# A last image gathered in four column parts, its row sums spread in float32r, and row sums transposed in bfloat16

## The reference

```
emb  = xn_flat @ dist_w.T                       # 1024 x 32
adj  = (24 nearest by distance) & (distance <= 10), or the diagonal
X    = xn_flat @ fc_w.T + fc_b
Dv   = row sums of adj;   De = column sums of adj
out  = (adj / De) @ adj.T / Dv @ X + xn_flat    # per image
o    = batch norm of out over all four images and all nodes, times gamma, plus beta
result = x + o * sigmoid(o)
```

## Time and profile before

| what | value |
|---|---|
| median of 3 runs | 173.52 us (173.44 to 174.02) |
| the profiled execution's own time | 173.63 us |
| its span (first to last instruction) | 171.8 us |
| busy: PE, DVE, ACT, POOL | 153.1, 143.6, 118.6, 105.7 us |
| mean granted TensorE clock | 0.974 of full speed |
| DMA | 17.72 MB, mean 103 GB/s |

### The profile page before, as it was taken

One profiled execution on the slowest core, in us unless ns is written; L12 is line 12 of the kernel. 1 busy time (PEld: TensorE's weight loads), 2 busy tenths in 40 slices (PEclk: granted clock), 3 DMA queues, 4 the chain that ended last, 5 costly groups with the idle time before them and its releaser, 6 DMA issues.

```text
span 171.8 us, 4074 instructions
## 1 busy us (share of the span) xinstructions
PE 153.1 (89%) x1235; PEld 98.9 (58%) x1237; DVE 143.6 (84%) x863; ACT 118.6 (69%) x199; POOL 105.7 (62%) x160
## 2 busy tenths in 40 slices
PE   6999999899989999899999989999999999999000
PEld 2334532444547665566666757667877778979000
DVE  0679999999996894999999999599769986588582
ACT  1257679998696996985578799649916574590590
POOL 1000556869975677399996479999619999380000
PEclk9999999999999999999999999999999999999955
DMA  5821000442937475309726070980641379994057
GB/s 191 264 111 2 2 4 0 63 74 52 121 68 126 51 77 109 78 12 200 113 52 122 4 123 4 214 154 6 122 92 37 62 184 95 148 338 163 0 208 280
DMA packets 42346, 17.72 MB, mean 103 GB/s; under 512 B 38832, under 2 KB 39496, under 8 KB 42320
## 3 DMA queue, kind: packets, MB, share of 16 engines
q1 hardware_dynamic: 41456, 17.03, 48.1%
q10 hardware_dynamic: 864, 0.40, 0.9%
HBM read 6.11 MB, written 2.13 MB: 48 GB/s over the span
## 4 chain that ended last, share of the span: by engine, by line
PE 72%; ACT 9%; DVE 6%; POOL 6%; issue 4%; ACTq 0%; DVEq 0%; POOLq 0%
PE pt L500 22%; PE pg L474 20%; PE po L533 10%; PE pt L562 5%; PE po L453 3%; ACT key L714 3%; PE po L431 3%; PE pt L533 2%; POOL x_wide L844 2%; DVE xn L1172 2%; PE po L440 2%; POOL tw L836 1%; ACT xn L800 1%; PE pg L555 1%; PE pg L453 1%
## 5 line engine op out<-in xcount | busy, mean ns | idle before, releaser
L982 DVE MAX8 cand<-key 128x8 f32<-128x64 f32 x512 | 78.1, 208 | 0.3
L500 PEld LDWEIGHTS pt<-xp,H 128*128 128x128 bf16 x768 | 44.4, 97 | 8.7 <-issue 7.6
L500 PE MATMUL pt<-xp,H 128*128 128x128 bf16 (+1 forms) x768 | 49.1, 220 | 0.1
L714 ACT ACTIVATE key<-pg 128x512 f32<-128x512 f32 x64 | 34.6, 594 | 19.1 <-PE pg L474 18.7
L474 PE MATMUL pg<-right,left 64*128 64x512 f32 x128 | 40.5, 641 | 3.1 <-ACT key L714 3.1
L881 POOL TENSOR_SCALAR H<-sign 128x1024 bf16<-128x1024 bf16 x32 | 33.4, 1043 | 13.1 <-ACT sign L722 13.1
L722 ACT ACTIVATE sign<-key,thr 128x1024 bf16<-128x1024 f32 x32 | 36.8, 1151 | 5.8 <-DVE thr L998 5.6
L474 PEld LDWEIGHTS pg<-right,left 64*128 64x128 f32 x128 | 12.5, 184 | 16.0 <-ACT key L714 8.0
L844 POOL CAST x_wide<-HT 128x1024 fp32r<-128x1024 bf16 x12 | 12.2, 1040 | 4.8 <-PE po L533 4.8
L562 PE MATMUL pt<-filler 128*128 128x512 bf16 x40 | 12.8, 450 | 1.4 <-POOL filler L805 1.3
L810 POOL TENSOR_SCALAR xn<-x_sb,gn_nm,gn_rs 128x1024 f32<-128x1024 f32 x3 | 3.6, 1194 | 16.4 <-DVE gn_rs L969 16.4
(11 more groups left out here) (96 smaller groups left out, 210.2 us busy)
## 6 DMA issues: line engine op xcount, KB each, us to landing
x_sb<-x SPq DMA_DIRECT2D x1, 2048.0 KB, 7.9
out<-xn SPq DMA_DIRECT2D x7, 256.0 KB, 2.1
dvb<-inv_rows SPq DMA_DIRECT2D x3, 512.0 KB, 4.5
x_sb<-x SPq DMA_DIRECT2D x1, 1024.0 KB, 6.4
left<-left SPq DMA_DIRECT2D x6, 128.0 KB, 2.3
x_sb<-x SPq DMA_DIRECT2D x1, 512.0 KB, 3.4
HT<-H SPq DMA_TRANSPOSE x32, 3.3
x_sb<-x ACTq DMA_DIRECT2D x1, 256.0 KB, 3.2
```

The source lines that it names most:

```text
L500: mm = pe.matmul(pt[:, j // T_BLOCKS, at:at + wide], lhs, x_cols(b, t, q, wide), start=(t == 0 and j % T_BLOCKS == 0 and q == 0), stop=(t ...
L714: act.activation(key[:, k % KEYS, cols], pg[:, h, :], ACT.Copy).then_inc(s["drained"], 1)
L982: ins = dve.max(cand[:, k % 2, c, :], key[:, k % KEYS, c * CHUNK:(c + 1) * CHUNK])
```

## The change

- The last image's gather has four parts of 256 columns. Part 0 goes to `po`, parts 1 to 3 to `pt`. Parts are taken in pairs: piece 0 of both, then piece 1 of both. Its T is scaled in four groups of 1, 2, 3 and 2 blocks.
- `spread_inverse` uses float32r: 1/Dv in two pieces that DVE makes (`invert_dv`, two operations more), by a float32r identity that POOL makes at the start: 16 matmuls for 8. ACT copies the result ahead of widening tiles 6 and 7, into `x32` (as `dvb_end`).
- `t_rest` of the last image goes from POOL to DVE, between `scale_t(3)` and `out_part(2, 1)`.
- Three `y_stats` move forward: (0, 1) into `limit(31)` ahead of the flag's read, (1, 0) ahead of the read of the last flag, (1, 1) between that flag's load to a register and the branch.
- For images 0 to 2 the row sums themselves are turned, as one bfloat16 matmul; DVE's `row_sums` is one operation where `invert_dv` had three, and `scale_t` has a maximum and a reciprocal on 8 x 128 where it had a copy.

```
-        T_GROUPS = [[[(0, 3), (3, 1)], [(4, 2), (6, 2)]]] * (B - 1) + [[[(0, 3)], [(3, 3)], [(6, 2)]]]
+        T_GROUPS = [[[(0, 3), (3, 1)], [(4, 2), (6, 2)]]] * (B - 1) + [[[(0, 1)], [(1, 2)], [(3, 3)], [(6, 2)]]]
...
         def parts(b):
-            return [(0, HALF), (HALF, 3 * HALF // 2), (3 * HALF // 2, N)] if b == B - 1 else [(0, HALF), (HALF, N)]
+            n = HALF // 2 if b == B - 1 else HALF
+            return [(a, a + n) for a in range(0, N, n)]
         def out_bank(b, i):
             a, z = parts(b)[i]
-            return (pt if b == B - 1 else po)[:, i, 0:z - a]
+            return (pt[:, i - 1, 0:z - a] if i > 0 else po[:, 0, 0:z - a]) if b == B - 1 else po[:, i, 0:z - a]
...
             def gather_order(b):
-                return [(part, q) for part in range(len(parts(b))) for q in range(T_PIECES)]
+                ahead = 2 if b == B - 1 else 1
+                return [(part + i, q) for part in range(0, len(parts(b)), ahead) for q in range(T_PIECES)
+                        for i in range(ahead)]
...
-                    if q == 0 and j == 0 and 0 < b < B - 1:
+                    if q == 0 and j == 0 and b > 0 and (b < B - 1 or part == 0):
                         pe.wait_ge(s["o_used"], 2 * (b - 1) + part + 1)
...
-            def turn_inverse(b):
-                pe.wait_ge(s["rdv_ready"], b + 1)
+            def turn_sums(b):
+                pe.wait_ge(s["dv_ready"], b + 1)
                 if b > 0:
                     pe.wait_ge(s["rows_made"], b)
-                pe.matmul(turned, rdv[:, b, :], cst[:, C_IDENT:C_IDENT + P], start=True, stop=True, skip_group_check=True)\
+                pe.matmul(turned, dv[:, :], ident_b[:, :], start=True, stop=True, skip_group_check=True)\
                     .then_inc(s["turned"], 1)
-            def spread_inverse(b):
-                pe.wait_ge(s["rdv_ready"], b + 1)
+            def spread_inverse():
+                pe.wait_ge(s["ident_made"], 1)
+                pe.wait_ge(s["rdv_split"], 2)
                 for h in range(2):
                     pe.wait_ge(s["drained"], 2 * (len(pair) - 1) + h + 1)
                     for i in range(TH):
                         t = h * TH + i
-                        mm = pe.matmul(pg[:, h, i * P:(i + 1) * P], rdv[:, b, t:t + 1].to_broadcast([P, P]),
-                                       cst[:, C_IDENT:C_IDENT + P], start=True, stop=True, skip_group_check=True)
+                        for q in range(2):
+                            mm = pe.matmul(pg[:, h, i * P:(i + 1) * P], rdv_w[:, q, t:t + 1].to_broadcast([P, P]),
+                                           ident_w[:, :], start=(i == 0 and q == 0), stop=(i == TH - 1 and q == 1),
+                                           skip_group_check=True)
                     mm.then_inc(s["spread"], 1)
...
+            spread_copy()
             for t in range(TILES - 2, TILES):
                 widen(B - 1, t)
-            spread_copy(B - 1)
...
+            pool.tensor_copy(ident_w[:, :], cst[:, C_IDENT:C_IDENT + P]).then_inc(s["ident_made"], 1)
...
-            t_rest(B - 1)
             residual(B - 2, 1)
...
+                if k == ALL - 1:
+                    y_stats(0, 1)
                 for g in RELEASE[k]:
                     read_flags(g)
...
                 under = dve.value_load(least_at(g).bitcast(I32))
+                if g == len(GROUPS) - 1:
+                    y_stats(1, 1)
                 dve.wait_ge(s["clipped"], GROUPS[g][-1] + 1)
...
-                    dve.tensor_copy(inv[:, :], turned).then_inc(s["rows_made"], 1)
+                    limited = signal(dve.tensor_scalar(inv[:, :], turned, DEG_EPS, None, ALU.max))
+                    dve.wait_ge(s["step"], limited)
+                    dve.reciprocal(inv[:, :], inv[:, :]).then_inc(s["rows_made"], 1)
...
+            def row_sums(b):
+                if b > 0:
+                    dve.wait_ge(s["turned"], b)
+                dve.tensor_scalar(dv[:, :], cs[:, b, :], -0.5, N / 2, ALU.mult, ALU.add).then_inc(s["dv_ready"], 1)
             def invert_dv(b):
...
-                dve.reciprocal(rdv[:, b, :], rdv[:, b, :]).then_inc(s["rdv_ready"], 1)
+                link(dve.reciprocal(rdv[:, :], rdv[:, :]))
+                dve.tensor_copy(rdv_w[:, 0, :], rdv[:, :]).then_inc(s["rdv_split"], 1)
+                dve.wait_ge(s["rdv_split"], 1)
+                dve.tensor_tensor(rdv_w[:, 1, :], rdv[:, :], rdv_w[:, 0, :].bitcast(F32), ALU.subtract)\
+                    .then_inc(s["rdv_split"], 1)
+            def t_rest(b):
+                for h, cols in halves():
+                    dve.wait_ge(s["t_hi"], 2 * b + t_before(b, h * TH + TH - 1))
+                    dve.tensor_tensor(tw[:, 1, cols], t32[:, cols], tw[:, 0, cols].bitcast(F32), ALU.subtract)\
+                        .then_inc(s["t_lo"], 1)
...
+            y_stats(1, 0)
             for g in RELEASE[ALL]:
                 read_flags(g)
                 release(g)
             invert_dv(B - 1)
             out_part(B - 2, 0)
             scale_t(B - 1)
+            t_rest(B - 1)
             out_part(B - 2, 1)
-            for b, h in ((0, 1), (1, 0), (1, 1), (2, 0)):
-                y_stats(b, h)
+            y_stats(2, 0)
             for i, (a, z) in enumerate(parts(B - 1)):
-                if i == 1:
+                if i == 2:
                     y_stats(2, 1)
```

More of the change, by code:

```diff
@@ L187, in build @@
         picked = sb("picked", [P, 1])
-        rdv = sb("rdv", [P, B, TILES])
+        dv = sb("dv", [P, TILES], BF16)
+        rdv = sb("rdv", [P, TILES])
+        rdv_w = sb("rdv_w", [P, 2, TILES], F32R)
+        ident_w = sb("ident_w", [P, P], F32R)
         inv = sb("inv", [TILES, P])
@@ L194, in build @@
         dvb = sb("dvb", [P, N])
+        dvb_end = x32
         prod = sb("prod", [P, 2, HALF])
         esq = prod
-        bn_st = sb("bn_st", [P, B * 2 + 1, 6])
+        bn_st = sb("bn_st", [P, B * 2 + 2, 6])
         bn_mv = sb("bn_mv", [P, 2])
@@ L211, in build @@
                  "x_lo limited signed lowered flagged flag_read clipped noise_made settled h_used t_scaled t_hi "
-                 "t_lo rdv_ready turned rows_made rdv_out dvb_in spread dvb_made o_ready o_used y_ready step slow_step stats_done bn_sd "
+                 "t_lo dv_ready rdv_split ident_made turned rows_made rdv_out dvb_in spread dvb_made o_ready o_used y_ready step slow_step stats_done bn_sd "
                  "bn_affine silu_done summed filler_set x_back").split()
@@ L302, in parts @@
         def parts(b):
-            return [(0, HALF), (HALF, 3 * HALF // 2), (3 * HALF // 2, N)] if b == B - 1 else [(0, HALF), (HALF, N)]
+            n = HALF // 2 if b == B - 1 else HALF
+            return [(a, a + n) for a in range(0, N, n)]
         def out_bank(b, i):
             a, z = parts(b)[i]
-            return (pt if b == B - 1 else po)[:, i, 0:z - a]
+            return (pt[:, i - 1, 0:z - a] if i > 0 else po[:, 0, 0:z - a]) if b == B - 1 else po[:, i, 0:z - a]
+        ENDS = [(0, HALF), (HALF, 3 * HALF // 2), (3 * HALF // 2, N)]
         SILUS = [(b, a, z) for b in range(B) for a, z in ([(0, HALF), (HALF, N)] if b == 0 else
-                                                          parts(b) if b == B - 1 else [(0, N)])]
-        SUMS = [(b, a, z) for b in range(B) for a, z in parts(b)]
+                                                          ENDS if b == B - 1 else [(0, N)])]
+        SUMS = [(b, a, z) for b in range(B) for a, z in (ENDS if b == B - 1 else parts(b))]
         def silus_before(b, z):
@@ L593, in _ @@
                     scatters(k)
-                    turn_inverse(b - 1)
+                    turn_sums(b - 1)
                 for j in FILL[k][:1]:
@@ L625, in _ @@
             scatter(23)
-            turn_inverse(2)
+            turn_sums(2)
             gather(1, 8)
@@ L643, in _ @@
             scatter(31)
-            spread_inverse(B - 1)
+            spread_inverse()
             gather(B - 1, len(parts(B - 1)) * T_PIECES * TILES)
@@ L741, in widen, with spread_copy @@
                                ACT.Copy).then_inc(widened[b][t // TH], 1)
-            def spread_copy(b):
-                act.wait_ge(s["o_used"], 2 * b)
+            def spread_copy():
+                act.wait_ge(s["x_lo"], 2 * B)
                 for h, cols in halves():
                     act.wait_ge(s["spread"], h + 1)
-                    act.activation(dvb[:, cols], pg[:, h, :], ACT.Copy).then_inc(s["dvb_made"], 1)
+                    act.activation(dvb_end[:, cols], pg[:, h, :], ACT.Copy).then_inc(s["dvb_made"], 1)
             def begin_image(k):
@@ L1071, in scale_t @@
                     ins.then_inc(s["t_scaled"], 1)
+            def row_sums(b):
+                if b > 0:
+                    dve.wait_ge(s["turned"], b)
+                dve.tensor_scalar(dv[:, :], cs[:, b, :], -0.5, N / 2, ALU.mult, ALU.add).then_inc(s["dv_ready"], 1)
             def invert_dv(b):
```

(11 more changed lines are left out.)

## The result

| | median | range, runs | ratio to before |
|---|---|---|---|
| before | 173.69 us | 173.24 to 174.02, 6 | |
| after | 175.32 us | 174.73 to 175.42, 6 | 1.0093, 95% interval 1.008 to 1.0107 |

What follows compares the result with a forecast made beforehand. The prediction took PE as the main bound, with DVE also busy in many loop windows. A loop gain of 0.45 and a tail loss of 0.8 gave +0.35 us: 173.9 us on the runs' scale, range 172.9 to 175.2.

Steps and rivals of the forecast that it cites:

- a tail loss of 0.8: After the loop: the last product starts at 159.7 instead of 158.93, behind DVE's statistics of part 2; 0.8 us lost.
- a loop gain of 0.45: Loop: three shorter turns save PE 0.6 us, of which the loop gains 0.45, from 0 to 0.8.
- the reciprocal in `scale_t`: Loop, DVE: a reciprocal on 8 x 128 was to take 0.20 to 0.35 us, 0.3 with its wait.
- the statistics that were to cost nothing ahead of tile 30's flag: DVE ahead of that flag's read: y_stats(0, 1) takes 0.69 us in an idle 0.74, so costs nothing.
- the delay of tile 31's release: Tail: the flag's read starts 0.59 us later, settled follows by 0.95; PE stalls 0.2, scatter(31) ends 0.3 later.
- As one or the other is the bound: Loop: PE or DVE bounds it, so it gains less than PE's 0.6 us; DVE gains 0.1 an image net.
- PE's hold at the turn: Loop, images 0 to 2: one bfloat16 matmul, turn to next matmul 0.1 to 0.15 us for 0.32.
- rival 1: Spread: float32r under 256 columns runs at the float32 rate, 0.23 us each, giving 175.1 us; chance 0.2.
- the waits of PE for blocks in the first quarters: Last gather: PE waits for T's blocks, idle some 0.5 us in all among the first 8 matmuls.
- the last product behind part 2's statistics: Tail end: DVE takes 1.245 us a part against PE's 0.96, so part 3's product starts 0.25 behind PE.
- `y_stats(1, 1)`: Tail, after the register load: starts at 147.45 and frees DVE at 148.05 instead of 147.13, +0.9 us.
- The rest on DVE: Last gather: the wait for POOL's rest, ready at 153.74 when PE wants it at 153.6, is gone.

Runs made afterwards that it cites:

- late_recip: The changed kernel with the reciprocal on 8 x 128 moved behind T's scaling; ratio to before 1.0053.
- back_10: The changed kernel with y_stats(1, 0) back in the tail, y_stats(1, 1) still between register load and branch; ratio to before 1.0034.
- undo_stats: The changed kernel with both statistics of image 1 back in the tail, behind image 2's last product; ratio to before 1.0019.

## Why the prediction was wrong

The forecast was +0.35 (a tail loss of 0.8 less a loop gain of 0.45); the trace has +1.35, the runs +1.6, above the top of the range. The direction and most of the tail's mechanisms were as told. Three terms of the sum were mis-sized: the reciprocal in `scale_t`, the statistics that were to cost nothing ahead of tile 30's flag, and the delay of tile 31's release. They make 0.9 of the 1.0 us between +0.35 and +1.35.

- **The reciprocal in `scale_t`**, taken at "0.3 with its wait": it took 0.94. My bounds came from forms of 8 values a partition and from a copy, and I counted it as one more small operation. With it ahead of T, PE's flag for tile 30 comes 0.13 earlier than before, and 0.40 earlier with it behind T: 0.27 of the miss. The Trainium skill (VectorE: DVE Perf Modes, "Walkthrough: the 8-slice pipeline in each mode") says that reciprocal is an iterative divide with a repeat count of 8. An estimate of 8 steps for each of 120 more values at its 0.96 GHz is 1.0 us over the short form; the trace has 0.94 - 0.20 = 0.74. The page doesn't say that every value takes eight steps; the estimate pointed the right way and went somewhat too far.
- **`y_stats(0, 1)`**, "takes 0.69 in an idle 0.74: nothing": the idle time was that of the kernel before, and what ends it is PE's flag, which the forecast itself let come 0.45 earlier. So the gap could not hold. In the changed kernel the read is 0.34 late and PE waits 0.34 before scatter(30). With this and the reciprocal the loop's gain of 0.45 became a loss of 0.12 at scatter(30) (125.03 for 124.91), together 0.57 of the miss.
- **"As one or the other is the bound"**: the late reciprocal shows that DVE's busy windows were not a bound there. What counted was what stood ahead of T's scaling. PE's hold at the turn (0.15 for 0.32) was as forecast, and so, with the reciprocal out of the way, was the loop's gain: 0.40 at the flag of tile 30 for 0.45. Only 0.16 of it is left at scatter(30) of `late_recip` (124.75 for 124.91), behind `y_stats(0, 1)`.
- **The release of tile 31**, where `settled` was to follow the read by 0.95 as before: the read came where expected (0.74 behind scatter(30)'s start for a forecast 0.62), but the register load took 0.87 for 0.52. scatter(31) stalled 0.57, not 0.2. Moving the load later moved it into tile 30's transposition. That is 0.35 of the miss.
- **Right:** `out_part(2, 0)` and then `scale_t` late on DVE's own account; the spread at 0.113, so that rival 1 (0.23 each) is out although its time, 175.1, was near the result: right number, wrong cause; the waits of PE for blocks in the first quarters; no wait for the rest; the last product behind part 2's statistics, 1.26 after the one before.
- **`y_stats(1, 1)`** was priced at 0.9 with (1, 0) ahead. Alone it costs nothing: most of it runs while DVE waits for tile 31 in any case, so that `invert_dv` starts 0.30 later in `back_10` than in `undo_stats` (126.42 for 126.12), and the idle 0.23 ahead of `scale_t` takes up the most of that. I hadn't priced the two statistics apart.
- **The rest on DVE** was told as a wait of PE that goes, 0.14 long (153.74 for 153.6); it was worth 0.54. This lay on the other side of the sum: with the rest on POOL the miss would have been larger.

## What to carry to other kernels

Filling an engine's idle time costs nothing only if the work is done before the signal that ends the idle time comes, and a change that speeds up the sender of that signal shrinks the gap: `y_stats(0, 1)` fitted the gap of the kernel before, and in the changed one it delayed the read of a flag by 0.34 us. `y_stats(1, 0)` of the same length had no gap at all ahead of a release and cost 0.74 us alone. Splitting a gather into finer parts makes its producer's cadence and the consumer's per-part time the bound: compare both with the time of a part before splitting. Price a reciprocal by its elements a partition, and put it behind whatever releases other engines.

## What the runs showed of the hardware

- A VectorE reciprocal took 0.203 us for 8 float32 values a partition (on 128 partitions) and 0.942 for 128 values (on 8 partitions), some 6 ns for each further value. A maximum on the same 8 x 128 took 0.227.
- float32r matmuls of 128 columns with a fresh 128 x 128 weight each run at 0.113 us, those of 256 columns at 0.120 and those of 512 at 0.231, at a granted clock of 1.00: under 256 columns the moving side no longer sets the rate. Two float32r matmuls cost what one float32 matmul does (two instructions at 0.115). A weight load took 0.19 us in float32r as in float32, and 0.10 in bfloat16.
- A load of one SBUF word into a VectorE register, that of tile 31's flag, took 0.52 us when it started 0.2 us behind the issue of tile 30's DMA transposition (six versions), 0.81 to 0.89 when it started 0.9 behind it (seven versions), and 0.52 again once the transposition was held back. The load of tile 30's flag took 0.68 to 0.82 in every version.
- At the start of each trace PE's matmuls of 512 columns ran 0.43 us apart and later 0.22, as at TensorE's two clock levels; that moment lay between 4.2 and 7.0 us after the first instruction. With it at 5.3 us the first threshold came at 20.87, with it at 7.0 at 21.45.
